# Scatters moved behind a step's seam, and thirteen VectorE operations a step moved or merged, in an mLSTM, attention and expert kernel

## What is computed

```python
lf = log_sigmoid(fg); lc = cumsum(lf)                  # gates, 8 heads
logD = where(mask, lc[..., :, None] - lc[..., None, :] + ig[..., None, :], -inf)
m = max(logD, -1); D = exp(logD - m)
Cmat = (q @ k.T) * D
norm = maximum(abs(Cmat.sum(-1)), exp(-m))
h = (Cmat / (norm + 1e-6)) @ v                         # then a layer norm over the 32 channels of a head
# attention: C[t] = sum over s<=t of softmax(e[s], s<=t) * H[s], t and s = the 4 images
# experts: top 2 of 8 by softmax; weights = the two probabilities over their sum; y = expert(x)
```

## Time and profile before

| | us |
|---|---|
| median of 3 runs (lowest, highest) | 660.44 (658.16, 663.61) |
| the profiled execution | 661.24 |
| its span, first to last instruction | 659.1 |
| busy PE / DVE / ACT / POOL | 504.9 / 434.3 / 338.7 / 253.1 |
| idle of POOL before scatters, waiting for DVE's slots | 65.9 |
| mean granted TensorE clock | 0.869 |

### The profile page before, as it was taken

How to read it: one execution, slowest core, us unless ns; L and a number is a source line. 1 busy time by engine, 2 the same in 40 slices (tenths; PEclk the granted TensorE clock), 3 DMA queues, 4 the chain that set the end, 5 groups by cost and what they waited for, 6 DMA issues and landing times. The chain is left out here.

```text
span 659.1 us, 13193 instructions
## 1 busy us (share of the span) xinstructions
PE 504.9 (77%) x3693; PEld 416.2 (63%) x3722; DVE 434.3 (66%) x1443; ACT 338.7 (51%) x887; POOL 253.1 (38%) x263
## 2 busy tenths in 40 slices
PE   5778999999998998897888933342029999999950
PEld 3455848687686875765766823232029999999950
DVE  7526546867796895894884938266545677776736
ACT  4464566575757665665565442252115555555530
POOL 7402021150513208308318173625634444444540
PEclk9676979999999999799899875756559999999995
DMA  7900000000000001001001010100122222222229
GB/s 161 288 1 0 2 0 1 1 1 1 1 1 1 1 2 33 0 1 34 1 1 33 2 33 0 33 9 29 52 70 53 62 66 66 67 62 62 64 66 339
DMA packets 34400, 28.06 MB, mean 43 GB/s; under 512 B 6775, under 2 KB 30089, under 8 KB 34352
## 3 DMA queue, kind: packets, MB, share of 16 engines
q1 hardware_dynamic: 24144, 16.38, 8.9%
q0 software_dynamic: 4320, 8.47, 3.9%
q10 hardware_dynamic: 5888, 2.62, 1.4%
HBM read 16.30 MB, written 11.61 MB: 42 GB/s over the span
## 5 line engine op out<-in xcount | busy, mean ns | idle before, releaser
L1773 POOL DMA_INDIRECT expert_rows<-xrow,slot x64 | 65.1, 1017 | 86.2 <-DVE slot L1489 65.9
L1287 DVE TENSOR_TENSOR PT<-pS,D 128x512 f32<-128x512 f32 x64 | 41.1, 684 | 44.6 <-PE pS L874 44.6
L899 PEld LDWEIGHTS pO<-vext,PT 128*128 128x128 f32 x512 | 64.1, 195 | 8.4 <-issue 3.8
L899 PE MATMUL pO<-vext,PT 128*128 128x99 f32 x512 | 65.5, 275 | 0.9 <-DVE PT L1287 0.8
L1765 POOL TENSOR_TENSOR var<-var,mhalf 128x16 f32<-128x16 f32 x16 | 48.6, 3041 | 45.8 <-DVE var L1319 45.4
L1765 POOL TENSOR_TENSOR rs<-rs,mhalf 128x4 f32<-128x4 f32 x16 | 17.6, 1101 | 101.4 <-DVE rs L1405 67.4
L726 ACT ACTIVATE sz<-pA,b1f 128x128 f32<-128x128 f32 x144 | 41.1, 368 | 29.8 <-PE pA L1095 29.8
L726 ACT ACTIVATE sx<-pS,b1f 128x128 f32<-128x128 f32 x140 | 40.0, 368 | 29.3 <-PE pS L1095 29.3
L550 ACT ACTIVATE D<-pA 128x512 f32<-128x512 f32 x64 | 36.8, 593 | 29.9 <-remote 16.6
L1815 POOL DMA_INDIRECT expert_out<-yT,vs x36 | 35.7, 992 | 40.2 <-DVE yT L1628 33.7
L1815 POOL DMA_INDIRECT expert_out<-yT,vext x35 | 34.2, 978 | 43.2 <-DVE yT L1628 42.5
(11 more groups left out here) (323 smaller groups left out, 1302.6 us busy)
## 6 DMA issues: line engine op xcount, KB each, us to landing
vs<-expert_rows SPq DMA_DIRECT2D x36, 65.0 KB, 1.8
vext<-expert_rows SPq DMA_DIRECT2D x35, 65.0 KB
x_tok<-in_x SPq DMA_DIRECT2D x8, 256.0 KB, 6.3
w<-in_L_ffn_W SPq DMA_DIRECT2D x1, 2048.0 KB, 10.3
w<-in_L_ffn_W SPq DMA_DIRECT2D x8, 256.0 KB, 6.9
xT<-expert_out SPq DMA_DIRECT2D x4, 512.0 KB, 5.3
out<-x_tok ACTq DMA_DIRECT2D x8, 256.0 KB, 6.2
expert_rows<-xrow,slot POOLq DMA_INDIRECT x64, 2.3
```

The lines of the kernel that those rows point to most:

```text
L899: last = mm(streamed(b, h % HPH), PT[:, h % 2, b, :], bc(vext2[t % 2][:, b, h, :], 1, COPIES), start=False, stop=(h % HPH == HPH - 1), ski ...
L1287: v.tensor_tensor(PT[:, h % 2].rearrange("p b i -> p (b i)"), pS[h % 2][:, :], D[:, h % 2].rearrange("p b i -> p (b i)"), ALU.mult).then_i ...
L1773: g.indirect_dma_start(xs, bass.IndirectOffsetOnAxis(slot[:, k, b:b + 1].bitcast(U32), 0), xrow[:, b, k, :], None).then_inc(sem(f"scattere ...
```

## The change

GpSimd: the scatters of tiles 0 to 3 leave the place after the routing in the same step and go to the next step, the first four behind `head_rstd` at its head, the other four behind the root of rs3. Those of tiles 4 to 7 go to the end of their own step, all eight together. `scatter` waits for `weights_in` and `rows_named` in place of `row_part`.

VectorE to ScalarE: `cexp` becomes four ACT copies scaled by `ofbatch_f` at the end of `gate_exps`; the absolute value of the normaliser's denominator becomes an ACT Abs in `square`; the names of the rows become one ACT operation in `send_rows`, with a table `rowbase` in place of a running `dest`. Merged without a new operation elsewhere: the negative part of the gate becomes a Relu in an activation that was there, the eps of the normaliser the bias of one in `gtok_copy`; the scans read the last column of the tile before in place of a copied carry (two `lc` buffers); the causal mask is added ahead of the maximum (`later4`); the slots are written as integers by the reduction. Per step DVE has 13 instructions fewer, ACT 7 more, POOL and PE as many as before. Three small operations each are new in the preparation on DVE and POOL.

```diff
@@ ACT
                 nc.scalar.activation(gm2[:, 1, :], fmin[:, :], ACT.Exp, scale=-1.0).then_inc(sem("gm2_done"), 1)
+                act.wait_ge(sem("parts_made"), t + 1)
+                for b in range(B):
+                    nc.scalar.activation(cexp2[t % 2][:, b, :], parts2[t % 2][:, 1, :], ACT.Copy,
+                                         scale=ofbatch_f[:, b:b + 1]).then_inc(sem("parts_ready"), 1)
...
             def square(t, f):
                 act.wait_ge(sem("half_copied"), 4 * t + 2 * f + 2)
+                after(act, "var_c", 2 * (t - 1) + f + 1)
+                nc.scalar.activation(nrm[:, f], osb[:, f, :, :, DH], ACT.Abs).then_inc(sem("den_turned"), 1)
...
                 act.wait_ge(sem("xt_ready"), B * s + B)
+                nc.scalar.activation(xrow[:, :, :, C + 1].bitcast(I32), dest[:, :, :], ACT.Identity,
+                                     bias=rowbase[:, s:s + 1]).then_inc(sem("rows_named"), 1)
@@ PE
-                    pe.wait_ge(sem("parts_ready"), t + 1)
+                    pe.wait_ge(sem("parts_ready"), B * (t + 1))
@@ DVE
             def gate(t):
-                    v.tensor_copy(rcar[:, 0:1], g32[(t - 1) % 2][0:BH, 1, P - 1:P]).then_inc(sem("gate_chain"), 1)
-                v.tensor_scalar(fmin[:, :], gpre[:, 1, :], 0.0, None, ALU.min
-                                ).then_inc(sem("gate_chain"), 1)
...
-                v.tensor_copy(lcar[:, :], lc[:, P - 1:P]).then_inc(sem("gate_chain"), 1)
...
-                v.tensor_tensor(cexp[:, :, :], bc(parts[:, 1, :], 1, B), bc(ofbatch[:, :], 2, P), ALU.mult
-                                ).then_inc(sem("parts_ready"), 1)
...
             def norm_a(t, f):
-                dve.wait_ge(sem("half_copied"), 4 * t + 2 * f + 2)
+                dve.wait_ge(sem("den_turned"), 2 * t + f + 1)
-                v.scalar_tensor_tensor(nrm[:, f], o[:, :, :, DH], -1.0, expm, ALU.mult, ALU.max
+                v.scalar_tensor_tensor(nrm[:, f], nrm[:, f], ROW_EPS, expm, ALU.add, ALU.max
                                        ).then_inc(sem("norm_taken"), 1)
-                v.tensor_tensor(nrm[:, f], nrm[:, f], o[:, :, :, DH], ALU.max).then_inc(sem("norm_chain"), 1)
-                v.tensor_scalar(nrm[:, f], nrm[:, f], ROW_EPS, (DH * LN_EPS) ** 0.5, ALU.add, ALU.mult
-                                ).then_inc(sem("norm_chain"), 1)
...
             def places_out(s):
-                v.tensor_copy(xrow[:, :, :, C + 1].bitcast(I32), dest[:, :, :]).then_inc(sem("row_part"), 1)
-                v.tensor_scalar(dest[:, :, :], dest[:, :, :], float(2 * B * P), None, ALU.add)
-                v.tensor_reduce(slotf[:, :, :], tmpk[:, :, :, :], AX.X, ALU.add).then_inc(sem("route_chain"), 1)
-                v.tensor_copy(slot[:, :, :], slotf[:, :, :]).then_inc(sem("slots_ready"), 1)
+                    v.tensor_reduce(slot[:, :, :], tmpk[:, :, :, :], AX.X, ALU.add).then_inc(sem("slots_ready"), 1)
@@ POOL
             def step(t):
+                five = 0 <= t - 5 <= T - 5
                 if one:
                     head_rstd(t - 1, 1)
+                if five:
+                    scatter(t - 5, (0,))
                 if three:
                     rsqrt(rs3[:, :], B, "var3_ready", t - 2, "rs3_ready")
-                if four:
-                    scatter(t - 4, (0,))
+                if five:
+                    scatter(t - 5, (1,))
                 if three:
                     row_scale(t - 3)
-                if four:
-                    scatter(t - 4, (1,))
                 if now:
                     skipped(t)
                 if one:
                     rsqrt(rs1[:, :], B, "var1_ready", t, "rs1_ready")
                 if now:
                     head_rstd(t, 0)
+                if four and t >= T:
+                    scatter(t - 4, (0, 1))
```

More of the change, by code:

```diff
@@ L191, in block_kernel @@
         lcar = sb("lcar", [BH, 1])
-        lc = sb("lc", [BH, P])
+        lc2 = [sb(f"lc{i}", [BH, P]) for i in range(2)]
         g32 = [sb(f"g3{i}", [96, 2, P]) for i in range(2)]
@@ L512, in gate_inputs @@
                                      ).then_inc(sem("fabs_done"), 1)
[L513 to L516, removed]
+                nc.scalar.activation(gpre[:, 0, :], bank[0:BH, 0:P], ACT.Identity, bias=bif[:, 0:1]
+                                     ).then_inc(sem("gpre_i_ready"), 1)
+                nc.scalar.activation(gpre[:, 1, :], bank[0:BH, P:2 * P], ACT.Relu, bias=negbf[:, 0:1], scale=-1.0
+                                     ).then_inc(read, 1)
                 act.wait_ge(sem("fabs_done"), t + 1)
@@ L530, in gate_exps @@
                 act.wait_ge(sem("c_ready"), t + 1)
-                nc.scalar.activation(uq[:, :], gc[:, 1, :], ACT.Exp, bias=rcar[:, 0:1], scale=-1.0
+                nc.scalar.activation(uq[:, :], gc[:, 1, :], ACT.Exp, bias=top_before(t), scale=-1.0
                                      ).then_inc(sem("uq_ready"), 1)
@@ L544, in gtok_copy @@
                 nc.scalar.activation(gtok2[t % 2][:, 1].rearrange("p b h -> p (b h)"), bank[:, BH:2 * BH],
-                                     ACT.Copy).then_inc(read, 1)
+                                     ACT.Identity, bias=roweps[:, 0:1]).then_inc(read, 1)
             def exps(t, h):
@@ L1149, in _ @@
             chain(v.memset(lcar[:, :], 0.0))
+            chain(v.memset(rcar[:, :], NEG))
+            chain(v.memset(roweps[:, :], ROW_EPS))
             for buf in xm2:
@@ L1207, in _ @@
             chain(v.tensor_scalar(vecs[:, 1], vecs[:, 1], float(DH) ** 0.5, None, ALU.mult))
+            chain(v.tensor_scalar(negbf[:, :], bif[:, 1:2], -1.0, None, ALU.mult))
             chain(v.tensor_copy(kg[:, 0, 0:P], ident[:, :]))
@@ L1232, in gate @@
             def gate(t):
-                g3, parts, cexp = g32[t % 2], parts2[t % 2], cexp2[t % 2]
+                g3, parts, lc = g32[t % 2], parts2[t % 2], lc2[t % 2]
                 gc = g3[0:BH]
@@ L1365, in softmax_in @@
                 bank, read = arrived(dve, s, "score")
-                v.tensor_copy(esc[:, :], bank[:, :].rearrange("p (b n) -> p b n", b=B)[:, :, 0]).then_inc(read, 1)
+                v.tensor_tensor(wat[:, :, :], bc(bank[:, :].rearrange("p (b n) -> p b n", b=B)[:, :, 0], 1, B),
+                                later4[:, :, :], ALU.add).then_inc(read, 1)
                 taken(dve, s, "score")
-                v.tensor_tensor_scan(emax[:, :], esc[:, :], esc[:, :], NEG, ALU.max, ALU.max
-                                     ).then_inc(sem("softmax_chain"), 1)
@@ L1485, in places_out @@
                                 ).then_inc(sem("route_chain"), 1)
[L1486 to L1489 removed]
+                dve.wait_ge(sem("route_chain"), 6 * s + 6)
+                with nc.allow_low_precision("whole numbers"):
+                    v.tensor_reduce(slot[:, :, :], tmpk[:, :, :, :], AX.X, ALU.add).then_inc(sem("slots_ready"), 1)
             for f in range(HALVES):
@@ L1736, in _ @@
             chain(g.tensor_copy(dest[:, :, :].rearrange("p b k -> p (b k)"), iota8[:, :]))
+            chain(g.iota(iota8[:, 0:T], [[2 * B * P, T]], 0, 0))
+            chain(g.tensor_copy(rowbase[:, :], iota8[:, 0:T]))
             chain(g.iota(iotat[:, :], [[1, MOE_TILES]], 0, 0))
@@ L1768, in scatter @@
                 pool.wait_ge(sem("slots_ready"), s + 1)
-                pool.wait_ge(sem("row_part"), 2 * (s + 1))
+                pool.wait_ge(sem("weights_in"), s + 1)
+                pool.wait_ge(sem("rows_named"), s + 1)
                 pool.wait_ge(sem("rows_scaled_out"), B * (s + 1))
@@ L1786, in step @@
                 now, nxt = t < T, t + 1 < T
-                one, three, four = 0 <= t - 1 < T, 0 <= t - 3 < T, 0 <= t - 4 < T
+                one, three, four, five = 0 <= t - 1 < T, 0 <= t - 3 < T, 0 <= t - 4 < T, 0 <= t - 5 <= T - 5
                 if nxt:
```

82 lines of the change are left out of this document (38 added, 44 removed).

## The result

The changed kernel takes 637.8 us (median of 4 runs, 634.3 to 642.8) against 660.0 us beside it: a ratio of 0.966, 95% interval 0.957 to 0.976. A second comparison on another occasion gave 641.7 against 661.2 us, 0.970 (0.965 to 0.974). The forecast was 643, range 630 to 654, faster.

The account below looks back on a forecast made before the run. TensorE bounds full steps, waits bound those from step 8; GpSimd's scatter order stalls 36.6 us. Terms 5.2 + 7.0 - 2.5 - 2.8 + 12.2 - 1.2 = 17.9 us off a 660.44 us median gave 643, range 630 to 654.

Parts of the forecast that it names:

- The seams: Seams 4|5 and 5|6: silu_x no longer waits behind GpSimd's scatters, gaining 5.2 and 7.0 us.
- The landing wait: Steps 5 and 6: ACT's send_rows waits 2.6 and 2.9 us for scatters to land, costing 2.5 and 2.8.
- the second rival: Steps 5 and 6: PE falls to the slow clock, costing 2.5 us each time, 648 us; chance 0.17.
- Step 7 on: From step 7 to the start of the last scatters: 10.2 + 1.2 + 0.8 = 12.2 us gained.
- The hold of 5.9 us: Step 7: ACT stands 5.9 us at send_rows until the scatters have landed.
- the 8 or more of step 8: Step 8: ACT's first xrow operation waits 8 us or more for the scatters' DMA.
- the slow products behind it: Step 7: PE's matmuls run at the slow clock after idling some 5 us, adding 3 us.
- The move's own share: Tail: DVE passes attn_bias 10.2 us earlier, and row_scale ahead of the scatters takes 1.2 us off the last chain.
- cexp on ACT: Steps 0 to 4: ACT's added work, with cexp reaching PE late, costs together 1.2 us.
- The edits off VectorE lie beside TensorE's work: Steps 0 to 7: some 2.5 us a step taken off DVE buys nothing by itself, as PE is full.
- ACT not held: Second four scatters land before ACT asks, so holds vanish: 624 us, or 634 with half the holds; chance 0.18.
- Slower scatters: Steps 5 to 8: scatters slow to about twice their pitch beside VectorE: 661 us, chance 0.12; slower, about 668, 0.05.

Follow-up runs that it names:

- e8: Changed kernel with two buffers of xrow and slot, and scatters one step late to the end; 622.7 against 661.2 us, ratio 0.940.
- e2: Kernel before with only GpSimd's new scatter order, VectorE and ScalarE as before; 641.8 against 660.8 us, ratio 0.971.
- e1: Changed kernel with GpSimd's scatters back in their old order, VectorE and ScalarE edits kept; 662.4 against 660.8 us, ratio 1.002.
- after again: Second profiled execution of the same changed kernel, no edit: span 642.6 us; its runs took 641.7 us, ratio 0.970.
- e11: Changed kernel, one buffer, with send_rows moved behind the square, q copies and masked state of the same step; 644.4 against 662.1 us, ratio 0.973.
- e5: Changed kernel with cexp made by one VectorE instruction again instead of four ACT copies; 638.4 against 661.2 us, ratio 0.966.
- e3: Changed kernel with all eight scatters of tile t-5 ahead of rs3 in steps 5 to 8; 629.1 against 660.8 us, ratio 0.952.
- e4: Changed kernel with two buffers each of xrow and slot, b2b sharing KVm's memory and loaded after step 7; 618.5 against 660.8 us, ratio 0.936.
- e10: Changed kernel with two buffers of xrow and slot, measured on another occasion; 622.5 against 662.1 us, ratio 0.941.

## Why the prediction was right, and where it was not

**The seams** (5.2 and 7.0). Right. Without the landing wait and at full clock steps 5 and 6 are 6.1 and 7.5 us shorter than in before (e8 against the first table). From `weigh` of head 0 to head 2, where I had read the 5.2, they are 5.3 and 7.3 us shorter; the half speed of the earlier trace rows lies between these heads and so within the 5.2. The rest lies behind: in step 5 it is 0.8, the size of the wait of `rows_turn` (0.84 in the earlier trace rows), which I had booked as recovered by the hold. It is not the hold that takes it away: it is still 0.84 in step 5 with the move alone (e2) and gone there with the edits alone (e1).

**The landing wait** (2.6 and 2.9 us of ACT, costing 2.5 and 2.8). Right in place, in its way to TensorE and nearly in size: 3.61 and 2.38 us, costing 3.2 and 3.2. I led it through the masked state, the gate exponentials and `cexp` to `exponents`, 3.1 us late in step 5; it is 3.2 late. What I missed is a stop on the way that costs nothing by itself: the q copies, whose bank `down` needs. `down` waits 2.31 us, but after again and e11 show that the time is lost at the gate columns whatever `down` does. Of the costs, the hold alone is 3.2 and 2.0 for my 2.5 and 2.8. The rest, 1.2 in step 6, is half speed: a part of the second rival's 2.5 was there in the forecast's own case, and in after again 1.5 and 1.6 us of it.

**Step 7 on** (12.2). The mechanism was right, the size low: 16.4. The hold of 5.9 us was 6.34, the 8 or more of step 8 were 14.54. Two terms were mis-sized. TensorE did idle some 5 us in step 7 (5.44), but the slow products behind it cost 0.9 us, not 3: `rows_turn` took 1.09 us for 0.66 and four products of the up projection 2.86 for 2.37. VectorE passes the seam 7|8 34.1 us into step 7, where the forecast had 36.8; so 2.7 of the 4.2 us above it are there already. And the small operations saved in the last steps, which I had put at 0.8 and a part of 1.6, are 3.4 by the edits alone (e1). The last scatter starts 26.1 us earlier than in before in the first profile and 16.9 in the second, where I had said some 18. The move's own share, 10.2 + 1.2 in the forecast, is 13.0 by e2. These shares are of one profile each.

**cexp on ACT** (-1.2). Mis-sized: steps 1 to 4 are 159.89 us in before and 159.79 after. Steps 2 and 3 are 0.2 and 0.4 longer, step 4 is 0.7 shorter, all at a clock of 1.00; putting it back moves step 3 by -0.49 and step 4 by +0.18 (e5).

**The edits off VectorE lie beside TensorE's work.** Right as far as the medians tell: ratio 1.002 alone, and no difference that can be measured beside the move. Step by step it is not quite so: step 4 is 0.7 us shorter, and the 0.8 us that `rows_turn` waited in step 5 are gone.

**Rivals.** ACT not held, forecast at 624, did not happen; made to happen it gave 629.1 (e3, held in step 8 still) and 618.5 and 622.5 (e4, e10). Slower scatters did not happen: 64 scatters of after took 954/959/1389 ns (min/median/max), and they landed 2.3 us after their start in the median, as in the earlier trace rows. The fivefold time that the Trainium skill gives for a DMA of GpSimd beside a VectorE copy (SBUF — State Buffer, section A bandwidth-pool intuition) is not seen in them. Nor was that case met: from 255 to 455 us of after no VectorE copy takes 0.3 us or more, and the `qprime` rows that the prediction calls copies are products.

**Left open.** What makes TensorE's clock fall in steps 0 and 4 of one execution and not of the next, whether the edits make it rarer in step 0; and whether the 3.4 us that e1 saved behind step 7 and lost in steps 5 and 6 were lost to the edits or to such stretches. No run here kept such stretches away.

## What to carry to other kernels

When a slow issue (here eight indirect DMAs, some 10 us) is moved behind a deadline, look for the next writer of the buffer that it reads: here the single row buffer kept back as much as the move gave, and a second one gave 19 to 23 us more. For an instruction that waits, list who takes over the PSUM banks of the instructions queued behind it as well as who reads their results; then ask which of these stops sets the time. The first stop that a trace shows need not be it: here e11 took away the wait of `down`, and TensorE waited further on. Operations taken off an engine that is not the bound are worth little until the chain behind reaches them; here that was from step 7 on.

## What the runs showed of the hardware

Two profiled executions of one kernel differed by 10.1 us, 8.3 of them in four steps in which TensorE's stretches of half speed stand or fall differently. Such a stretch cost up to 3.9 us (step 0), and nothing where it fell into a wait (`down` in step 5). The stretches stand at places that recur from kernel to kernel (about 87 to 97 us, 202 to 212, 247 to 257) but not in every execution. What the engine did just before did not tell the two cases apart where I looked: in step 5 `down` ran at half speed in after and at full speed in after again, behind idle times of 2.31 and 2.30 us. In step 0 of after again and of after (timelines of PE) both had waited as long, 0.42 us:

```profile
88.51 0.74 PE L859 MATMUL pG<-uq,spread 96*128 96x128 bf16 x8 [0.42 <-DVE uq L1277]
...
92.47 5.38 PE L821 MATMUL pG<-xT,wupT 128*128 128x512 f32 x8
```

```profile
87.02 0.62 PE L859 MATMUL pG<-uq,spread 96*128 96x128 bf16 x8 [0.42 <-DVE uq L1277]
...
89.60 3.80 PE L821 MATMUL pG<-xT,wupT 128*128 128x512 f32 x8
```

The same eight products take 5.38 us in one and 3.80 in the other. A gain of a few us read from two profiles means something only stage by stage, between stages of full granted clock; at a lower one it also counts which products the half speed fell on.
